# GpSimd holds the first batch's row transfers until the router logits of both batches are made

## The reference

```python
x = L0_attn_content
x = _layernorm(x + _L0_attn_ref(x, ...), axis=-1)
# _L0_ffn_ref, with h = x.reshape(4096, 256):
logits = jnp.einsum('th,eh->te', h, router_weight)
probs = softmax(logits); topk_probs, selected = top_k(probs, 2)
# slot: the rank of a (token, expert) pair in its expert; kept if slot < 1280
expert_inputs = zeros(8 * 1280 + 1, 256).at[dispatch].set(h[st])
pre = einsum('ech,edh->ecd', ...); gate = einsum('ech,edh->ecd', ...)
expert_out = einsum('ecd,ehd->ech', pre * silu(gate), ...)
out = zeros(T, 256).at[st].add(expert_out[dispatch] * kept_w)
x = _layernorm(x + out)
```

## Time and profile before

| what | us |
|---|---|
| median of 3 runs | 1915.46 |
| lowest and highest run | 1907.22 and 1916.75 |
| span of the profiled execution | 1938.8 |
| of it: projections and attention | up to about 1100 |
| of it: routing block | about 1100 to 1255 |
| of it: experts | about 1255 to 1904 |
| of it: last layernorm and store | about 1904 to the end |

### The profile page before, as it was taken

One profiled execution on the slowest core, in us unless ns is written; L12 is line 12 of the kernel. 1 busy time (PEld: TensorE's weight loads), 2 busy tenths in 40 slices (PEclk: granted clock), 3 DMA queues, 4 the chain that ended last, 5 costly groups with the idle time before them and its releaser, 6 DMA issues. The chain is left out here.

```text
span 1938.8 us, 31529 instructions
## 1 busy us (share of the span) xinstructions
PE 1658.6 (86%) x10758; PEld 1025.6 (53%) x10759; DVE 1151.0 (59%) x2219; ACT 1268.4 (65%) x1416; POOL 251.4 (13%) x251
## 2 busy tenths in 40 slices
PE   7848999999999999999999742099999999999990
PEld 6623433333333333334333442078988988889880
DVE  6855767768677676676877642045354444554533
ACT  7748999999999999999999710024233333332422
POOL 0000000000000000000000033612111221131111
PEclk9969999999999999999999855589999999999995
DMA  5577010100101101011010121333131412322016
GB/s 174 175 206 234 17 33 16 33 26 23 33 16 33 28 22 33 18 31 30 20 33 16 40 98 50 105 121 89 35 101 16 115 52 67 105 65 63 12 12 183
DMA packets 91081, 124.92 MB, mean 64 GB/s; under 512 B 10240, under 2 KB 76544, under 8 KB 91008
## 3 DMA queue, kind: packets, MB, share of 16 engines
q1 hardware_dynamic: 76416, 106.85, 17.4%
q0 software_dynamic: 14592, 17.06, 4.8%
HBM read 74.78 MB, written 51.18 MB: 65 GB/s over the span
## 5 line engine op out<-in xcount | busy, mean ns | idle before, releaser
L697 ACT ACTIVATE probs<-scores 128x1536 f32<-128x1536 f32 (+1 forms) x384 | 520.6, 1379 | 48.7 <-PE scores L627 43.5
L627 PE MATMUL scores<-aq,ak 98*128 98x512 bf16 (+3 forms) x1280 | 304.1, 352 | 61.5 <-DMA aq<-shift_dram 26.8
L740 DVE TENSOR_REDUCE sums<-expq 128x1 f32<-128x1408 f32 (+6 forms) x448 | 347.3, 827 | 13.8 <-ACT expq L703 13.8
L643 PE MATMUL o_ps<-probs,vh 128*32 128x512 f32 (+3 forms) x2560 | 340.0, 543 | 0.0
L1386 ACT ACTIVATE gate<-up_ps 128x512 f32<-128x512 f32 x128 | 76.5, 598 | 350.8 <-PE up_ps L1278 348.6
L627 PE MATMUL scores<-ak,aq 98*128 98x512 bf16 (+3 forms) x1184 | 264.5, 343 | 17.0 <-ACT probs L697 9.0
L703 ACT ACTIVATE expq<-scores 128x1536 f32<-128x1536 f32 x192 | 274.8, 1449 | 2.0
L627 PEld LDWEIGHTS scores<-aq,ak 98*128 98x128 bf16 x1280 | 96.8, 98 | 235.4 <-ACT probs L697 72.8
L627 PEld LDWEIGHTS scores<-ak,aq 98*128 98x128 bf16 x1184 | 91.2, 98 | 238.5 <-ACT expq L703 94.7
L727 DVE TENSOR_TENSOR hidden<-probs,after 128x384 f32<-128x384 f32 x128 | 70.9, 554 | 243.9 <-ACT probs L697 243.9
L1278 PE MATMUL up_ps<-xeT_hi,wup_hi 128*128 128x512 f32 x512 | 205.7, 402 | 11.4 <-issue 9.9
(11 more groups left out here) (209 smaller groups left out, 2378.8 us busy)
## 6 DMA issues: line engine op xcount, KB each, us to landing
raw<-w_T SPq DMA_DIRECT2D x16, 1024.0 KB, 10.0
split_dram<-parts SPq DMA_DIRECT2D x48, 256.0 KB, 2.9
aq<-split_dram SPq DMA_DIRECT2D x192, 64.0 KB
xe_dram<-blank SPq DMA_DIRECT2D x1, 10560.0 KB, 56.1
raw<-wg_T SPq DMA_DIRECT2D x8, 1024.0 KB, 8.7
xin<-xe_dram SPq DMA_DIRECT2D x8, 792.0 KB, 5.5
ak<-split_dram SPq DMA_DIRECT2D x32, 192.0 KB
xin<-xe_dram SPq DMA_DIRECT2D x8, 528.0 KB, 3.8
```

The costliest lines, as they stand in the source:

```text
L627: last = nc.tensor.matmul(dst[:, at:at + w], still, moving[0:KS, lo:lo + w], start=True, stop=True, skip_group_check=True)
L643: last = nc.tensor.matmul(dst[32 * r:32 * r + 32, BLK - w:BLK], vh[j % 2][:, k, :], probs[:, m % P_RING, at:at + w], start=first, stop=Tru ...
L697: last = nc.scalar.activation(probs[:, m % P_RING, 0:w], src[:, 0:w], ACT.Exp, scale=HD ** -0.5)
L740: last = nc.vector.tensor_reduce(sums[:, j % 2, col:col + 1], expq[:, n % X_RING, at:at + w], AX.X, ALU.add)
```

## The change

One wait is put in front of GpSimd's loop over the batches. It asks for `lg_ready` at B x GB = 8, which the last logits matmul of the second batch brings. Nothing else is changed, and no buffer, order or count of transfers is.

```diff
                 pool.wait_ge(iota_ready, 7)
                 pool.wait_ge(xe_cleared, 16)
+                pool.wait_ge(lg_ready, B * GB)
                 for b in range(B):
                     pool.wait_ge(rows_ready, b + 1)
                     send(of_batch(b))
```

## The result

| | before | changed |
|---|---|---|
| median of 4 runs, us | 1912.14 | 1938.97 |
| lowest and highest | 1907.22 to 1916.75 | 1933.83 to 1944.78 |
| span of the profiled execution | 1938.8 | 1936.7 |

The ratio is 1.014, with a 95% interval of 1.0111 to 1.017: the change costs 26.8 us. The forecast was 1942, which was 26.5 us above the median known then, 1915.46; one more run has moved that to 1912.14.

The account below looks back on a forecast made before the run. The prediction took POOL's last send to bound the routing block. Holding that the runs lack the 26.0 us stall, it added the 27.1 us late start to the 1915.46 median: 1942.6, stated as 1942, range 1914 to 1948.

Parts of the forecast that it names:

- The bound: Routing block: its end is set by POOL's last send; 8.5 us follow until the experts block starts.
- When the wait opens: Second batch's logits on PE: ready between 1161.7 and 1167.8, taken as 1165, with the first send at 1166.1.
- The sum of the trace: POOL's sends in the profiled execution: +27.1 - 26.0 = +1.1 us, giving a span of 1939.9.
- the late start: POOL's first send, held by the new wait, comes 27.1 us later than before.
- the gap that closes: POOL's idle between its two trains of 32 sends: 26.0 us of extra idle gone, one joined train.
- What stands for before: Timed runs of before: taken to lack the 26.0 us stall, so their median rises by 27.1 to 1942.6.
- the crawl: PE's slow stretch beside the first train of row transfers, in the second batch's routing; costs 26.0 us on the path.
- rival B: PE between 1151 and 1184: the runs crawl too, because of the first train; the change removes it, 1916.6; chance 0.20.
- Rival C: Second batch's logits: the crawl comes of something else, as the 2 MB store, and stays; 1943.8; chance 0.06.
- my two arguments against it: Against the store as cause: PE busy 4.00 of 4 us beside the first store; DVE's copy 4.57 us late at 1155.47.
- The estimate by the 6.2 us: Profile total above run time by 6.2 us: only 17 of 23 us would be stall, loss 18 us, near 1933.
- That trace recording throttles PE: PE in the profiled execution: the block writing trace records could hold back engines, making the crawl a price of recording.

Follow-up runs that it names:

- after_third: The changed kernel once more beside the kernel before, on chip 9: 1941.72 us against 1940.60, ratio 1.0003.
- before_again: The kernel before, an unchanged second copy, on chip 15: 1937.10 us against 1941.14, ratio 0.9983.
- wait_mid: The kernel before with the new wait only ahead of the second batch's train, on chip 15: 1940.35 us, ratio 0.9996.
- hold_store_2: The kernel before with SP's second-batch store waiting for all eight groups of logits, on chip 9: 1941.13 us against 1940.60, ratio 1.0001.
- half_wait: The kernel before with the wait after the first 16 sends: 1925.53 us, ratio 0.9924 on chip 15; 1923.12 us, ratio 0.9913 on chip 9.
- wait_20_again: The kernel before with the wait ahead of the 21st send, on chip 13: 1922.33 us against 1941.84, ratio 0.9902.
- wait_20: The kernel before with the wait ahead of the 21st send, on chip 8: 1913.67 us against 1913.14, ratio 1.0007.
- hold_store: The kernel before with SP's second-batch store waiting for all eight groups of logits, on chip 11: 1912.78 us against 1913.83, ratio 0.9996.
- wait_six: The changed kernel's wait asking for 6 groups instead of 8, against the kernel before on chip 15: 1934.08 us, ratio 0.9966.

## Why the prediction was right, and where its reason was wrong

**The bound: right.** The block ends with POOL's last send. In every trace 8.5 us lie between the last send and the experts block. What comes after that is not quite constant: from the start of the experts block to the end of the span it is 680.3 to 686.1 us in the traces, with the same work in each, so two single spans can be compared only to some 6 us.

**When the wait opens: right.** I took the logits at 1165, the first send at 1166.1 and the last send's end at 1247.8. They were 1164.2, 1165.3 and 1247.0. The second dest, taken at 1178.2, was ready at 1177.6.

**The sum of the trace: right.** +27.1 for the late start, -26.0 for the gap that closes. On chips that crawl (after_third, chip 9) the two cancel: ratio 1.0003, 1.1 us more. The span after came out at 1936.7, not 1939.9; 2.4 of the 3.2 us lie in the experts and after (1936.7 - 1255.48 = 681.2 against 1938.8 - 1255.23 = 683.6), where nothing was changed.

**What stands for before: the right number for a reason that was half wrong.** The step was "I therefore hold that the crawl belongs to the profiled execution and hardly to the runs". The runs of the first comparison indeed held none, and that decides the result: rival B would have given 1916.6. But that the trace was a profiled execution is not what sets it apart. The crawl goes with the chip (or the sitting on it). On chips 9, 13 and 15 all 55 runs of before lie between 1931.6 and 1944.7 us, on chips 8 and 11 all 34 between 1906.6 and 1916.7, and no run of one sitting falls among those of the other kind. Traces of kernels whose first train meets the second batch's matmuls show the crawl on chips 9, 13 and 15 (before_again, wait_mid, hold_store_2, and cut short in half_wait and wait_20_again) and none on 8 and 11 (wait_20, hold_store). So the profiled execution of before most likely came from a chip that crawls and the timed runs from one that doesn't; which chips they were isn't on record. What I read rightly was only that a span 23 us above the median means that the trace shows something the runs don't. That the runs came from a chip without the crawl was luck: beside the runs of before on chip 9 the change loses 1.1 us, which is the sum of rival B, and no reason of the prediction tells these two cases apart.

So rival B was not refuted; it is what happens on chip 9, where the changed kernel was run, and by the runs of before it would on 13 and 15. Its price, 26.0 us, comes out as 25.9 us between the trains of hold_store on chips 11 and 9, and as 26.8 between the runs of before there (1940.6 - 1913.8). One of the prediction's readings for it was off: PE doesn't recover within 3 us of the last send. That send ended at 1179.86, and the 32 matmuls at full pace start at 1185.21, 5.4 us later.

**Rival C is refuted** by the changed kernel's trace, where the logits come at 1164, and the store as the cause by hold_store_2. Of my two arguments against it the first was sound, the store of the first batch beside PE at 4.00 of 4 us. The second, the late copy at 1155.47, proves less: it was due at 1151.1, and the store moves from about 1152 on (the DMA engines carry 87 GB/s from 1150 to 1152 and 333 from 1152 to 1154), so most of its lateness lies beside the store. It is hold_store_2 that has the same late copy, at 1155.04 after 5.28 us of idle, with no store beside it.

**The pages.** The estimate by the 6.2 us of the Trainium skill's "Runtime: NRT & Kernel Launch" (a loss of 18 us) was laid on the wrong quantity. The page, in its section on the preamble and postamble, speaks of a profile's total; the span here runs from the first to the last instruction, and a run takes 1.8 us more than it. That trace recording throttles PE, the idea drawn from the Trainium skill's "NOTIFIC — the notification-queue block" (on the write path), isn't enough by itself: the traces on chips 8 and 11 were recorded too and don't crawl. On the other chips it isn't excluded, since no run there is known to be without recording.

**What stays open** is why PE crawls on one chip and not on another. It takes more than indirect transfers beside PE: the trace of before crawls in the routing block, yet from 1305 to 1315 PE is busy for 10.00 of 10 us beside GpSimd's adds of the experts block. It isn't the granted clock: that is at 0.50 both in the crawl and from 1185.2 on, where 32 matmuls take 6.96 us. It starts late: in half_wait, wait_20_again and hold_store_2 the first two turns and 16 logits are issued at their usual pace, but the second copy of hT comes 2.0 to 5.0 us late (the first turn's start + 3.65 is when it is due), 14 to 17 us after the first send, and the last 32 logits of wait_six, beside a train that has just begun, aren't slowed.

And it is not only a slow pace. In the trace of before the third turn of the second batch ends at 1154.06 by its row, before any matmul is slowed, but the copy that waits for it and for the first group's logits comes at 1184.37, together with the one for the fourth turn. In before_again the last turn starts at 1176.54, and both copies come at 1183.59. So signals of finished matmuls reach DVE and ACT up to 30 us late, and in before_again the last 7 us of the stall are such a wait. In the four full crawls traced (before, before_again, wait_mid, hold_store_2) the two copies come 5.1 to 5.5 us after the start of the train's last send. Whether the slow pace and the late signals are one thing, no run here tells.

## What to carry to other kernels

A stall that a trace shows can be removed and bring nothing, if the cure starts the bounding queue later by as much as the stall held it up: write down both ends of that queue, not the stall. Place such a wait where it is already fulfilled, or nearly, in the good case. Here, ahead of the 21st send, it costs nothing measurable on a chip without the crawl (1.0007) and takes 19.5 us off on one with it (0.9902), while ahead of the first send it loses 24.7 to 26.8 us without the crawl and wins nothing with it. And when a profiled span doesn't fit between the runs, find out whether both were taken on the same chip before reasoning from the trace.

## What the runs showed of the hardware

On three of five chips (each in one sitting) a train of indirect row transfers from GpSimd (135 KB each, one per 1.28 us, 103 GB/s) makes TensorE start these float32 matmuls only every 0.70 us or a multiple of it (hold_store_2), instead of every 0.22 us, although the DMA engines are busy for 0.29 of the time. The signals of its finished matmuls come late as well, by up to 30 us in the trace of before. The copies of DVE and ACT take 0.69 and 0.60 us in the crawl as they do without it, and GpSimd keeps its 1.28 us. Full pace is back 2 to 5.5 us after the last send ends (half_wait, before).
